# Attention with values split into halves: the low halves from a TensorE product and a ScalarE copy instead of a VectorE subtraction

## Chip, cores and metric

One core of one Trainium2 chip. The metric is the device time of one execution in microseconds (us), the median of several runs. The engines of the core are named as the profile does: PE (TensorE), DVE (VectorE), ACT (ScalarE), POOL (GpSimd), SP (SyncE).

## What is computed

The reference runs four blocks on x of shape (4, 2048, 256); the second and fourth are the same feed-forward block, the third is the attention that the change is in:

```python
x = x + attn_a(layernorm(x))          # row 1 of each sequence, one 256x256 product, broadcast
x = x + ffn(layernorm(x))             # sigmoid(xr Wr) * (relu(xk Wk)^2 Wv), x mixed with the row before
x = x + attn_b(layernorm(x))          # below
x = x + ffn(layernorm(x))
# attn_b: 16 heads of 64, windows of 128 rows
q, k, v = rope(proj(Wq, bq)), rope(proj(Wk, bk)), proj(Wv, bv)
kcat, vcat = (window before, own window)
scores = q kcat^T / 8, masked to kj >= qi and kj <= qi + 128
ctx = softmax(scores) vcat
out = merged(ctx) Wo^T + bo
```

Products of float32 values are made from float16 halves: a value is split into a high half (rounded to float16) and a low half (what is left, again float16), and three products (high-high, high-low, low-high) are summed in PSUM. The values v are such a case. The high half is `v_h`, the low half `v_l = v - v_h`.

## The kernel before

The kernel has three stages on one core: a feed-forward stage (which also prepares the attention's weights), the attention, and a second feed-forward stage. Everything is ordered by hand: every engine has a function `at_step(t)` that lists its pieces in the order in which it issues them, and semaphores alone tie the engines together. Each engine runs its list strictly in order, so a wait holds up all that stands behind it.

The attention has 64 steps t. A step is one group of 4 heads (g = t % 4) for one big block S = t // 4 of 4 x 128 rows; 16 big blocks make 4 sequences of 4. For a step and each block b of its four, the pieces are:

- queries and keys: `project` on PE (L1580) into one of the two banks `pr_ps[:, half]`; then the rotary products by `key_product`, `query_product` (DVE L1341, L1351 and POOL), the copies `key_copy`, `query_copy` (ACT L1504, L1514), and the sums on POOL (L1171, L1181).
- values: `values` on PE (L1597) into the same two banks, `v_high_of` on ACT (L1475) writes the high half, `v_low_of` on DVE (L1330) the low half. Both read the bank.
- scores on PE (L1685), `tops` on DVE (L1256, masks the scores and takes the maximum of a row), `exponentials` on ACT (L1457), `p_high_of` on ACT (L1466) and `p_low_of` on DVE (L1268) for the halves of the probabilities, a DMA transpose (`turn_p`, L1061), `values_product` on PE (L1638 to L1640), `context` on DVE (L1277, L1283).
- context: `context_high` on ACT (L1495), its low half on POOL (L1202), a DMA transpose (L1069), `output` on PE (L1654, L1657), `residual` on DVE (L1320).
- every fourth step: row statistics on DVE (`moments`, in steps with g = 1 and g = 3), and with g = 3 `normalize` and `x_high_of` on ACT (L1522, L1533) and `x_low_of` on DVE (L1312) for the block after next.

In step t the engines work on the scores of step t, on values and queries of step t + 1, and on keys of step t + 2. The two banks `pr_ps[:, 0]` and `pr_ps[:, 1]` are shared: queries, then values, then keys go through both. `keys_of(t + 2, half)` may overwrite a bank only when the low half of the values has been read from it:

```python
def keys_of(t, half):
    ...
    pe.wait_ge(xt_in[r], xt_ready(t // NG))
    need(v_low[half], t)
    project(r, KC + t % NG * 2 * P, half, k_done[half])
```

The order of PE in `at_step(t)` around it is: values of t + 1, `values_product(t - 1, 3)`, `output(t - 5)`, `values_product(t, 0)`, `keys_of(t + 2, 1)`, `scores(t + 1, 0)`, `keys_of(t + 2, 0)`, `values_product(t, 1)`. DVE's is: `tops(t, 3)`, `context(t - 1, 3)`, `v_low_of(t + 1, 1)`, `residual(t - 5)`, `v_low_of(t + 1, 0)`, `context(t, 0)`, two key products of t + 2 (they wait for `keys_of(t + 2, 1)`), `p_low_of(t, 2)`, `p_low_of(t, 3)`. ACT's is: `exponentials(t, 3)`, with g = 3 `normalize` and `x_high_of`, `p_high_of(t, 3)`, `context_high(t - 1)`, `key_copy(t + 2)`.

Of the kernel before, what the change touches and what calls it, by code (L numbers as in the profile page):

```python
# [57 lines left out]
def identity(nc, pool, tile, made, n=1):  # L58
# [21 lines left out]
             "kt": F + 57376, "prob": F + 69664, "v_h": F + 77856, "v_l": F + 84096, "halves": F + 90240,  # L80
             "pt": F + 106624, "c_halves": F + 114816, "tables": D, "masks": D + 8192, "rows": D + 10240,
             "bias_parts": D + 10496, "out_bias": D + 11008}
# [784 lines left out]
def attention_stage(nc, stack, x_in, x_out, place, banks, pre, past, bv, bo, cos, sin):  # L867
# [34 lines left out]
    out_bias = sb("out_bias", [P, C])  # L902
    masks = sb("masks", [P, 2 * P])
    rows = sb("rows", [P, P], BF16)
    bias_parts = sb("bias_parts", [P, C], BF16)
# [61 lines left out]
    k_carried = sem("k_carried")  # L967
    v_high = [sem("v_first_high"), sem("v_second_high")]
    v_low = [sem("v_first_low"), sem("v_second_low")]
    s_done = sem("s_done")  # L970
# [13 lines left out]

    MASKS_MADE, MADE = 5, 6
    OUT_BIAS_MADE = 11
# [155 lines left out]
    def gpsimd(pool):  # L1142
# [62 lines left out]
        def opening():  # L1205
# [8 lines left out]
            for half, rule in enumerate((beyond, until)):  # L1214
                part = masks[:, half * P:(half + 1) * P]
                nc.gpsimd.affine_select(out=part, in_=part, **rule).then_inc(made, 1)

        def first_std():
# [25 lines left out]
    def vector(dve):  # L1244
# [77 lines left out]

        def v_low_of(t, half):

            if step(t):
                dve.wait_ge(v_high[half], t + 1)
                if t < 2:
                    dve.wait_ge(past.act_made, 2 * past.CHUNKS)
                at = pair_of(t, half)
                nc.vector.tensor_tensor(v_l[:, at, :, :],  # L1330
                                        pr_ps[:, half, :].rearrange("p (b h d) -> p b h d", b=2, d=HD),
                                        v_h[:, at, :, 0:HD], ALU.subtract).then_inc(v_low[half], 1)

        def key_product(t, n):
# [58 lines left out]
        def at_step(t):  # L1393
# [15 lines left out]
            context(t - 1, 3)  # L1409
            v_low_of(t + 1, 1)  # L1410
            if g == 3 and S > -2:
                shift_of(S + 2)
            residual(t - 5)
            v_low_of(t + 1, 0)
            context(t, 0)
# [31 lines left out]
    def scalar(act):  # L1447
# [21 lines left out]
        def v_high_of(t, half):  # L1469

            if step(t):
                act.wait_ge(v_done[half], t + 1)
                need(pv_done, 4 * t - 4)
                at = pair_of(t, half)
                nc.scalar.activation(v_h[:, at, :, 0:HD],  # L1475
                                     pr_ps[:, half, :].rearrange("p (b h d) -> p b h d", b=2, d=HD),
                                     ACT.Copy).then_inc(v_high[half], 1)

        def carry_keys(t):
# [59 lines left out]
        def at_step(t):  # L1539
# [14 lines left out]
            if g == 3 and S > -2:  # L1554
                x_high_of(S + 2)
            p_high_of(t, 3)
            context_high(t - 1)
            key_copy(t + 2)
# [3 lines left out]
    def tensor(pe):  # L1562
# [22 lines left out]
        def values(t, half):  # L1585

            if step(t):
# [6 lines left out]
                for blk in range(2):  # L1594
                    for n, (xp, wp) in enumerate(TERMS):
                        for k in range(CK):
                            last = nc.tensor.matmul(  # L1597
                                pr_ps[:, half, blk * 2 * P:(blk + 1) * 2 * P], xt[:, r, xp, 2 * half + blk, k, :],
                                w[wp][:, k, VC + g * 2 * P:VC + (g + 1) * 2 * P],
                                start=n == 0 and k == 0, stop=n == 2 and k == CK - 1)  # L1600
                last.then_inc(v_done[half], 1)

        def keys_of(t, half):
# [87 lines left out]
        def at_step(t):  # L1691
# [6 lines left out]
            values_product(t - 1, 3)  # L1698
            output(t - 5)
            values_product(t, 0)  # L1700
            keys_of(t + 2, 1)
# [207 lines left out]
```

## Time and profile before

| | |
|---|---|
| median of 3 runs | 1657.75 us (1651.25 to 1658.65) |
| profiled execution | 1650.62 us |
| its span | 1648.8 us |
| its mean granted clock of PE | 0.981 |
| PE, PE's weight loads | 1487.5 us (90%), 1125.5 us (68%) |
| DVE | 1458.6 us (88%) |
| ACT | 1262.6 us (77%) |
| POOL | 967.5 us (59%) |

The span is what the profiler saw between first and last instruction; the profiled execution's own time is 1.8 us longer. Busy times are shares of the whole span, in which the attention takes about the stretch from 210 to 1450 us. A group of instructions carries a count, its busy time, the mean of one, and the idle time of its engine just before it with what ended it. In an order of time a row with x4 is four instructions run together. The durations of two instructions in a row can overlap a little, so a distance between starts is often the better measure.

### The profile page before, as it was taken

The numbers are of one execution on the slowest core, as the hardware profiler recorded it, in microseconds if no ns is written. First come the engines' busy times: TensorE is split into PE (matmuls) and PEld (weight loads), VectorE is DVE, ScalarE is ACT, GpSimd is POOL, SyncE is SP. The second block draws the span as 40 slices with busy tenths as digits, with TensorE's granted clock in tenths as the row PEclk, the third lists the DMA queues.
The fourth block names the chain that finished last, engine by engine and source line by source line (L and its number), as shares of the span: only waits on it lengthen the run. The fifth ranks groups of instructions, "written<-read, shape, count | busy, mean of one in ns | idle before, by whom it ended". The sixth has DMA issues, their size and how long they took to land. (4 is left out here: it accounts for less than half of the span.)

```text
span 1648.8 us, 46118 instructions
## 1 busy us (share of the span) xinstructions
PE 1487.5 (90%) x16674; PEld 1125.5 (68%) x16674; DVE 1458.6 (88%) x4009; ACT 1262.6 (77%) x2266; POOL 967.5 (59%) x786
## 2 busy tenths in 40 slices
PE   5999978899989999999989999999998999869998
PEld 4888745566666676666667666666666666658887
DVE  5999588899989999999999999999999989957885
ACT  5999567777767787877777877778787767749996
POOL 4665357565656666656666665666676656513443
PEclk7999999999999999999999999999999999979999
DMA  5233247899899989899999989899999798971331
GB/s 208 91 121 106 77 91 129 163 152 180 147 175 157 179 164 179 163 169 171 166 180 156 183 155 181 151 181 164 179 159 176 155 154 153 171 169 61 111 112 73
DMA packets 721528, 247.86 MB, mean 150 GB/s; under 512 B 687380, under 2 KB 706072, under 8 KB 721304
## 3 DMA queue, kind: packets, MB, share of 16 engines
q1 hardware_dynamic: 720600, 244.53, 76.4%
q8 instruction: 135, 2.21, 0.5%
q14 instruction: 89, 0.73, 0.1%
q10 hardware_dynamic: 704, 0.40, 0.1%
HBM read 47.73 MB, written 25.17 MB: 44 GB/s over the span
## 5 line engine op out<-in xcount | busy, mean ns | idle before, releaser
L1457 ACT ACTIVATE at_prob<-at_prob,at_top 128x256 f32<-128x256 f32 (+1 forms) x1024 | 429.0, 490 | 104.4 <-DVE at_top L1256 101.1
L1256 DVE CUSTOM_DVE_ANT_0 at_prob<-banks,at_masks,pre_s_scale 128x256 f32<-128x256 f32 (+1 forms) x1024 | 420.3, 470 | 16.2 <-PE banks L1685 1.9
L1268 DVE TENSOR_TENSOR at_halves<-at_prob,at_halves 128x1024 f16<-128x1024 f32 (+1 forms) x256 | 306.2, 1212 | 0.7 <-ACT at_halves L1466 0.7
L1580 PE MATMUL banks<-at_xt,pre_w_h 128*128 128x512 f16 x1024 | 297.9, 383 | 4.8 <-DVE at_v_l L1330 4.2
L1685 PE MATMUL banks<-at_kt,at_qt 32*128 32x256 f32 (+1 forms) x4096 | 253.8, 384 | 52.1 <-DVE at_top L1256 21.1
L1202 POOL TENSOR_TENSOR at_c_halves<-at_ctx,at_c_halves 128x1024 f16<-128x1024 f32 x64 | 136.6, 2135 | 267.0 <-DVE at_halves L1268 261.4
L1685 PEld LDWEIGHTS banks<-at_kt,at_qt 32*128 32x128 f32 x4096 | 202.5, 187 | 112.8 <-issue 110.5
L1466 ACT ACTIVATE at_halves<-at_prob 128x1024 f16<-128x1024 f32 (+1 forms) x256 | 263.6, 1030 | 7.7
L1638 PE MATMUL banks<-at_v_h,at_pt 128*128 128x65 f16 x1984 | 208.0, 195 | 49.8 <-DMA at_pt<-at_halves 32.8
L1638 PEld LDWEIGHTS banks<-at_v_h,at_pt 128*128 128x128 f16 x1984 | 181.1, 97 | 104.1 <-issue 49.3
L1171 POOL TENSOR_TENSOR at_kt<-at_k_by 128x512 f32<-128x512 f32 x128 | 163.0, 1274 | 94.4 <-DVE at_halves L1268 94.3
L1161 POOL TENSOR_TENSOR at_q_by<-at_q_first,at_tables 128x512 f32<-128x512 f32 x128 | 163.1, 1275 | 81.0 <-DVE at_halves L1268 81.0
L1639 PE MATMUL banks<-at_v_l,at_pt 128*128 128x64 f16 x1984 | 207.6, 193 | 0.0
L1640 PE MATMUL banks<-at_v_h,at_pt 128*128 128x65 f16 x1984 | 207.4, 194 | 0.0
L1639 PEld LDWEIGHTS banks<-at_v_l,at_pt 128*128 128x128 f16 x1984 | 182.1, 99 | 6.8
L1504 ACT ACTIVATE at_k_first<-banks,pre_bias 128x512 f32<-128x512 f32 x64 | 44.0, 687 | 186.2 <-PE banks L1580 186.2
L1640 PEld LDWEIGHTS banks<-at_v_h,at_pt 128*128 128x128 f16 x1984 | 182.5, 98 | 0.0
L325 POOL TENSOR_TENSOR f_x<-f_x,f_gated 128x512 f32<-128x512 f32 x64 | 83.1, 1308 | 156.1 <-DVE f_gated L430 156.1
L1151 POOL TENSOR_TENSOR at_k_by<-at_k_first,at_tables 128x512 f32<-128x512 f32 x128 | 160.5, 1276 | 13.8 <-ACT at_k_first L1504 13.8
L1597 PE MATMUL banks<-pre_w_h,at_xt 128*128 128x256 f16 x1024 | 164.1, 273 | 0.8 <-ACT at_q_first L1514 0.8
L1181 POOL TENSOR_TENSOR at_qt<-at_q_by 128x512 f32<-128x512 f32 x128 | 160.2, 1273 | 0.0
L1580 PEld LDWEIGHTS banks<-at_xt,pre_w_h 128*128 128x128 f16 x1024 | 87.1, 98 | 104.7 <-issue 28.8
(124 smaller groups left out, 3221.0 us busy)
## 6 DMA issues: line engine op xcount, KB each, us to landing
f_x<-in_x SPq DMA_DIRECT2D x16, 512.0 KB, 4.0
x_after_ffn<-f_x SPq DMA_DIRECT2D x16, 512.0 KB, 2.6
at_x_ln<-x_after_ffn SPq DMA_DIRECT2D x16, 512.0 KB, 4.7
at_x_res<-x_after_ffn SPq DMA_DIRECT2D x64, 128.0 KB, 2.9
x_after_attention<-at_x_res SPq DMA_DIRECT2D x64, 128.0 KB, 2.7
f_x<-x_after_attention SPq DMA_DIRECT2D x16, 512.0 KB, 4.3
out_x<-f_x SPq DMA_DIRECT2D x16, 512.0 KB, 3.0
at_tables<-in_cos SPq DMA_DIRECT2D x16, 256.0 KB, 3.7
```

The costliest lines, as they stand in the source:

```text
L1161: nc.gpsimd.tensor_tensor(q_by[:, n, :], q_first[:, :], tables[:, r, n // 3, :], ALU.mult).then_inc(q_made[n], 1)
L1171: nc.gpsimd.tensor_tensor(kt[:, half, own(t, 0):own(t, 0) + SB, :].rearrange("p s t -> p (s t)"), k_by[:, 2 * half, :], k_by[:, 2 * half + ...
L1256: last = nc.vector.tensor_tensor_reduce(out=prob[:, n % 2, h, low:2 * P], in0=s_ps[:, h, n % 2 * 2 * P + low:(n % 2 + 1) * 2 * P], in1=mas ...
L1268: nc.vector.tensor_tensor(parts[:, 1, :, :], prob[:, n % 2, :, keys_from(t, b):2 * P], parts[:, 0, :, :], ALU.subtract).then_inc(p_low, 1)
L1457: last = nc.scalar.activation(at, at, ACT.Exp, bias=top[:, n % 2, h:h + 1], scale=-1.0)
L1466: nc.scalar.activation(halves_of(n, alone(t, b))[:, 0, :, :], prob[:, n % 2, :, keys_from(t, b):2 * P], ACT.Copy).then_inc(p_high, 1)
L1580: last = nc.tensor.matmul(pr_ps[:, half, :].rearrange("p (b t) -> p b t", b=SB), w[wp][:, k, at:at + P], xt[:, r, xp, :, k, :], start=n == ...
L1597: last = nc.tensor.matmul(pr_ps[:, half, blk * 2 * P:(blk + 1) * 2 * P], xt[:, r, xp, 2 * half + blk, k, :], w[wp][:, k, VC + g * 2 * P:VC ...
L1638: nc.tensor.matmul(out, ph, v_h[:, at, h, :], start=s == 0, stop=False)
L1639: nc.tensor.matmul(out[:, 0:HD], ph, v_l[:, at, h, :], start=False, stop=False)
L1640: last = nc.tensor.matmul(out, pl, v_h[:, at, h, :], start=False, stop=s == len(slots) - 1)
L1685: last = nc.tensor.matmul(s_ps[:, h, d * 2 * P + keys_from(t, b):(d + 1) * 2 * P] .rearrange("p (s t) -> p s t", t=P), qt[rows_of, par, ha ...
```

## The change

The low half is made by PE in the bank itself: after the values' sum has been copied out as `v_h`, a product of minus the identity (`neg_eye`, float16, made once on POOL) with `v_h` is added to the same sum, so that the bank holds v - v_h. ACT then copies the bank to `v_l`. The subtraction on DVE is gone. `values` no longer closes its sum, and starts it only once for the bank.

```diff
+    neg_eye = sb("neg_eye", [P, P], F16)
...
+    v_rest = [sem("v_first_rest"), sem("v_second_rest")]
...
-    MASKS_MADE, MADE = 5, 6
+    MASKS_MADE, EYE_MADE, MADE = 5, 7, 8
...
+            nc.gpsimd.memset(neg_eye[:, :], 0.0).then_inc(made, 1)
+            pool.wait_ge(made, EYE_MADE - 1)
+            nc.gpsimd.affine_select(out=neg_eye[:, :], in_=neg_eye[:, :], compare_op=ALU.not_equal, fill=-1.0, base=0,
+                                    pattern=[[-1, P]], channel_multiplier=1).then_inc(made, 1)
...
-        def v_low_of(t, half):
-
-            if step(t):
-                dve.wait_ge(v_high[half], t + 1)
...
-                nc.vector.tensor_tensor(v_l[:, at, :, :],
-                                        pr_ps[:, half, :].rearrange("p (b h d) -> p b h d", b=2, d=HD),
-                                        v_h[:, at, :, 0:HD], ALU.subtract).then_inc(v_low[half], 1)
...
             context(t - 1, 3)
-            v_low_of(t + 1, 1)
             if g == 3 and S > -2:
                 shift_of(S + 2)
             residual(t - 5)
-            v_low_of(t + 1, 0)
             context(t, 0)
...
+        def v_low_of(t, half):
+
+            if step(t):
+                act.wait_ge(v_rest[half], t + 1)
...
+                nc.scalar.activation(v_l[:, pair_of(t, half), :, :],
+                                     pr_ps[:, half, :].rearrange("p (b h d) -> p b h d", b=2, d=HD),
+                                     ACT.Copy).then_inc(v_low[half], 1)
...
             p_high_of(t, 3)
+            v_low_of(t + 1, 1)
+            v_low_of(t + 1, 0)
             context_high(t - 1)
             key_copy(t + 2)
...
-                                start=n == 0 and k == 0, stop=n == 2 and k == CK - 1)
+                                start=blk == 0 and n == 0 and k == 0, stop=False, skip_group_check=True)
...
+        def values_rest(t, half):
+
+            if step(t):
+                pe.wait_ge(v_high[half], t + 1)
...
+                for blk in range(2):
+                    last = nc.tensor.matmul(
+                        pr_ps[:, half, blk * 2 * P:(blk + 1) * 2 * P].rearrange("p (h d) -> p h d", d=HD),
+                        neg_eye[:, :], v_h[:, valued(t, 2 * half + blk), :, 0:HD], start=False, stop=blk == 1,
+                        skip_group_check=True)
+                last.then_inc(v_rest[half], 1)
...
             output(t - 5)
+            values_rest(t + 1, 1)
+            values_rest(t + 1, 0)
             values_product(t, 0)
             keys_of(t + 2, 1)
```

How the order of the instructions moves, with the semaphores that each waits for. ACT in a step with g = 3, before (L1457 exponentials, L1522 and L1533 x, L1466 high half of block 3, L1495 context, L1504 keys):

```order
L1457 ACTIVATE at_prob<-at_prob,at_top 128x256 [waits at_top_made]
L1457 ACTIVATE at_prob<-at_prob,at_top 128x256 x3
L1522 ACTIVATE at_x_ln<-at_x_ln,at_shift,at_rstd 128x256 [waits at_shift_made]
L1522 ACTIVATE at_x_ln<-at_x_ln,at_shift,at_rstd 128x256 x3
L1533 ACTIVATE at_x_halves<-at_x_ln 128x1024 [waits at_xt_in0,at_xn_made]
L1466 ACTIVATE at_halves<-at_prob 128x1024 [waits at_pt_in1,at_p_made]
L1495 ACTIVATE at_c_halves<-at_ctx 128x1024 [waits at_ct_in,at_ctx_made]
L1504 ACTIVATE at_k_first<-banks,pre_bias 128x512 [waits at_k_product3,at_k_product0,at_k_first_done]
```

And the same place of the change, whose lines have other numbers (the low halves are L1478):

```order
L1450 ACTIVATE at_prob<-at_prob,at_top 128x256 [waits at_top_made]
L1450 ACTIVATE at_prob<-at_prob,at_top 128x256 x3
L1525 ACTIVATE at_x_ln<-at_x_ln,at_shift,at_rstd 128x256 [waits at_shift_made]
L1525 ACTIVATE at_x_ln<-at_x_ln,at_shift,at_rstd 128x256 x3
L1536 ACTIVATE at_x_halves<-at_x_ln 128x1024 [waits at_xt_in0,at_xn_made]
L1459 ACTIVATE at_halves<-at_prob 128x1024 [waits at_pt_in1,at_p_made]
L1478 ACTIVATE at_v_l<-banks 128x2x256 [waits at_v_second_rest]
L1478 ACTIVATE at_v_l<-banks 128x512 [waits at_v_first_rest]
L1498 ACTIVATE at_c_halves<-at_ctx 128x1024 [waits at_ct_in,at_ctx_made]
L1507 ACTIVATE at_k_first<-banks,pre_bias 128x512 [waits at_k_product3,at_k_product0,at_k_first_done]
```

The two copies stand behind the high half of block 3, and in such a step behind the normalizing too; nothing else moved. PE from the output to the keys' first projection, before; the rest of the context's products is left out:

```order
L1657 MATMUL banks<-pre_wo_h,pre_raw 128x256 x8
L1638 MATMUL banks<-at_v_h,at_pt 128x65 [waits at_v_second_low,at_ctx_made,at_v_first_low,at_pt_in0]
L1639 MATMUL banks<-at_v_l,at_pt 128x64
L1640 MATMUL banks<-at_v_h,at_pt 128x65
...
L1580 MATMUL banks<-at_xt,pre_w_h 128x512 [waits at_v_second_low,at_xt_in1]
```

The same place of the change (L1675 is the output, L1656 to L1658 are the context's products):

```order
L1675 MATMUL banks<-pre_wo_h,pre_raw 128x256 x8
L1675 MATMUL banks<-pre_wo_l,pre_raw 128x256 x8
L1675 MATMUL banks<-pre_wo_h,pre_raw 128x256 x8
L1615 MATMUL banks<-at_v_h,at_neg_eye 128x256 [waits at_v_second_high]
L1615 MATMUL banks<-at_v_h,at_neg_eye 128x256
L1615 MATMUL banks<-at_v_h,at_neg_eye 128x256 [waits at_v_first_high]
L1615 MATMUL banks<-at_v_h,at_neg_eye 128x256
L1656 MATMUL banks<-at_v_h,at_pt 128x65 [waits at_v_second_low,at_ctx_made,at_v_first_low,at_pt_in0]
L1657 MATMUL banks<-at_v_l,at_pt 128x64
L1658 MATMUL banks<-at_v_h,at_pt 128x65
...
L1585 MATMUL banks<-at_xt,pre_w_h 128x512 [waits at_v_second_low,at_xt_in1]
```

Four products are put in ahead of the context's products; the keys' projection waits for the same semaphore as before, which ACT now raises. On DVE the key products follow the context of block 0 as before, without the two subtractions:

```order
L1289 TENSOR_TENSOR at_ctx<-banks,at_inv 128x256 [waits at_ct_low,at_inv_made]
L1326 SCALAR_TENSOR_TENSOR at_x_res<-banks,pre_o_down,at_x_res 128x256 [waits at_res_in0,at_o_done]
L1283 RECIPROCAL at_inv<-banks 128x4 [waits at_pv_done]
L1289 TENSOR_TENSOR at_ctx<-banks,at_inv 128x256 [waits at_ct_low,at_inv_made]
L1336 SCALAR_TENSOR_TENSOR at_k_by<-banks,pre_bias,at_tables 128x512 [waits at_k_first_roped,at_k_second_done,at_tab_in0]
L1336 SCALAR_TENSOR_TENSOR at_k_by<-banks,pre_bias,at_tables 128x512 [waits at_k_second_roped,at_k_second_done,at_tab_in0]
L1274 TENSOR_TENSOR at_halves<-at_prob,at_halves 128x1024 [waits at_p_high] x2
```

The key products (L1336) still wait for the keys' projection into the second bank, and the last two low halves of the probabilities (L1274) stand behind them.

## Rows read from the trace of the kernel before

**Rows 1.** The page, first part: busy time, share and instructions of each engine.
```profile
PE 1487.5 (90%) x16674; PEld 1125.5 (68%) x16674; DVE 1458.6 (88%) x4009; ACT 1262.6 (77%) x2266; POOL 967.5 (59%) x786
```

**Rows 2.** Busy time by stretch (start:end, length, each engine, PEclk, DMA share, GB/s).
```profile
700.00:900.00 200.00, 183.77 (x2382) 132.26 (x2384) 188.06 (x558) 150.06 (x275) 127.33 (x98) 1.00 0.95 167
```

**Rows 3.** Waits of PE and DVE, 220 to 1430 us: us in total, times, longest.
```profile
PE banks L1638 <- DMA at_pt<-at_halves: 29.7, 29, 3.4
PE banks L1580 <- DVE at_v_l L1330: 2.7, 1, 2.7
...
DVE at_k_by L1341 <- PE banks L1580: 21.6, 46, 2.0
```

**Rows 4.** The two tiles of the halves: min/median/max ns, first and last start.
```profile
L1330 DVE TENSOR_TENSOR at_v_l<-banks,at_v_h x128: 672/679/692, 210.1 to 1431.0; 128x512 f16<-128x512 f32 x128
...
L1475 ACT ACTIVATE at_v_h<-banks x128: 580/590/599, 209.5 to 1429.1; 128x512 f16<-128x512 f32 x128
```

**Rows 5.** Order of time on DVE around 738 us (start, length, line).
```profile
737.51 0.68 DVE L1330 TENSOR_TENSOR at_v_l<-banks,at_v_h 128x512 f16<-128x512 f32 x1
...
738.50 0.68 DVE L1330 TENSOR_TENSOR at_v_l<-banks,at_v_h 128x512 f16<-128x512 f32 x1
...
740.01 1.41 DVE L1341 SCALAR_TENSOR_TENSOR at_k_by<-banks,pre_bias,at_tables 128x512 f32<-128x512 f32 x2 [0.28 <-PE banks L1580]
```

**Rows 6.** Order of time on ACT, the same step.
```profile
737.07 1.71 ACT L1457 ACTIVATE at_prob<-at_prob,at_top 128x256 f32<-128x256 f32 x4
738.81 1.06 ACT L1466 ACTIVATE at_halves<-at_prob 128x1024 f16<-128x1024 f32 x1
739.77 1.04 ACT L1495 ACTIVATE at_c_halves<-at_ctx 128x1024 f16<-128x1024 f32 x1
```

**Rows 7.** Order of time on PE, the same step: output, then the keys.
```profile
735.77 1.04 PE L1657 MATMUL banks<-pre_wo_l,pre_raw 128*128 128x256 f16 x8
736.64 1.04 PE L1657 MATMUL banks<-pre_wo_h,pre_raw 128*128 128x256 f16 x8
...
738.45 0.60 PE L1580 MATMUL banks<-at_xt,pre_w_h 128*128 128x512 f16 x2
```

**Rows 8.** DVE: key products of single steps, and statistics of two rows.
```profile
680.86 1.41 DVE L1341 SCALAR_TENSOR_TENSOR at_k_by<-banks,pre_bias,at_tables 128x512 f32<-128x512 f32 x2
...
700.40 1.41 DVE L1341 SCALAR_TENSOR_TENSOR at_k_by<-banks,pre_bias,at_tables 128x512 f32<-128x512 f32 x2 [0.29 <-PE banks L1580]
...
711.19 0.75 DVE L1292 BATCH_NORM_STATS2 at_stats<-at_x_ln 128x6 f32<-128x256 f32 x2
...
711.97 0.25 DVE L1297 BATCH_NORM_AGGREGATE at_mv<-at_stats 128x2 f32<-128x6 f32 x2
...
721.61 1.41 DVE L1341 SCALAR_TENSOR_TENSOR at_k_by<-banks,pre_bias,at_tables 128x512 f32<-128x512 f32 x2 [0.44 <-PE banks L1580]
...
759.11 1.41 DVE L1341 SCALAR_TENSOR_TENSOR at_k_by<-banks,pre_bias,at_tables 128x512 f32<-128x512 f32 x2
...
875.40 1.41 DVE L1341 SCALAR_TENSOR_TENSOR at_k_by<-banks,pre_bias,at_tables 128x512 f32<-128x512 f32 x2
```

**Rows 9.** ACT: the last high half of single steps.
```profile
699.20 1.06 ACT L1466 ACTIVATE at_halves<-at_prob 128x1024 f16<-128x1024 f32 x1
...
719.23 1.06 ACT L1466 ACTIVATE at_halves<-at_prob 128x1024 f16<-128x1024 f32 x1
...
760.84 1.04 ACT L1466 ACTIVATE at_halves<-at_prob 128x1024 f16<-128x1024 f32 x1
...
891.60 1.06 ACT L1466 ACTIVATE at_halves<-at_prob 128x1024 f16<-128x1024 f32 x1
```

**Rows 10.** The line of the key products, 210 to 1440 us.
```profile
L1341 DVE SCALAR_TENSOR_TENSOR at_k_by<-banks,pre_bias,at_tables x126: 735/743/753, 213.0 to 1414.8; 128x512 f32<-128x512 f32 x126
```

**Rows 11.** Busy time by stretch, where the clock falls.
```profile
1328.00:1332.00 4.00, 1.82 (x33) 1.36 (x30) 3.79 (x15) 3.85 (x9) 2.84 (x3) 1.00 1.40 203
1332.00:1336.00 4.00, 3.10 (x15) 2.25 (x16) 0.98 (x2) 3.57 (x6) 3.01 (x3) 0.58 0.92 215
```

More of the change, by code:

```diff
@@ L80 @@
              "kt": F + 57376, "prob": F + 69664, "v_h": F + 77856, "v_l": F + 84096, "halves": F + 90240,
-             "pt": F + 106624, "c_halves": F + 114816, "tables": D, "masks": D + 8192, "rows": D + 10240,
+             "pt": F + 106624, "c_halves": F + 114816, "tables": D, "masks": D + 8192, "neg_eye": D + 9216, "rows": D + 10240,
              "bias_parts": D + 10496, "out_bias": D + 11008}
@@ L1321, in residual @@
                                                x_res[:, i % RB, :], ALU.mult, ALU.add).then_inc(x_made, 1)
-        def v_low_of(t, half):
-            if step(t):
-                dve.wait_ge(v_high[half], t + 1)
-                if t < 2:
-                    dve.wait_ge(past.act_made, 2 * past.CHUNKS)
-                at = pair_of(t, half)
-                nc.vector.tensor_tensor(v_l[:, at, :, :],
-                                        pr_ps[:, half, :].rearrange("p (b h d) -> p b h d", b=2, d=HD),
-                                        v_h[:, at, :, 0:HD], ALU.subtract).then_inc(v_low[half], 1)
         def key_product(t, n):
@@ L1477, in v_high_of @@
                                      ACT.Copy).then_inc(v_high[half], 1)
+        def v_low_of(t, half):
+            if step(t):
+                act.wait_ge(v_rest[half], t + 1)
+                if t < 2:
+                    act.wait_ge(past.act_made, 2 * past.CHUNKS)
+                nc.scalar.activation(v_l[:, pair_of(t, half), :, :],
+                                     pr_ps[:, half, :].rearrange("p (b h d) -> p b h d", b=2, d=HD),
+                                     ACT.Copy).then_inc(v_low[half], 1)
         def carry_keys(t):
@@ L1599, in values @@
                                 w[wp][:, k, VC + g * 2 * P:VC + (g + 1) * 2 * P],
-                                start=n == 0 and k == 0, stop=n == 2 and k == CK - 1)
+                                start=blk == 0 and n == 0 and k == 0, stop=False, skip_group_check=True)
                 last.then_inc(v_done[half], 1)
+        def values_rest(t, half):
+            if step(t):
+                pe.wait_ge(v_high[half], t + 1)
+                if t == 0:
+                    pe.wait_ge(made, EYE_MADE)
+                for blk in range(2):
[4 more added lines that the diff above has]
+                last.then_inc(v_rest[half], 1)
         def keys_of(t, half):
```

## Prediction

> **What bounds the kernel now.** I read the page's busy times first, then a stretch of the attention, then the waits, and last the order of time inside single steps. On the page TensorE (PE) and VectorE (DVE) are close, 90% and 88% of the span; ScalarE (ACT) has 77% [rows 1]. Inside the attention, of 200 us PE works 184, DVE 188, ACT 150 [rows 2]: VectorE is the fullest, PE next. PE's waits end mostly on DMA transposes of the probabilities (29.7 us), and only once, for 2.7 us, on the low halves of the values; DVE's longest wait, 21.6 us, is for the keys' projection [rows 3]. Two engines are nearly full, so the question is which ring of waits closes first when work leaves one of them.
>
> The ring to look at runs through the accumulation banks: the keys of the step after next are projected into the bank that the values have just left. In the quiet step around 738 us DVE writes the second half's low part at 737.51 and the first half's at 738.50, and its key product starts at 740.01 [rows 5]. PE starts the last products of the output at 736.64 and the keys' first projection at 738.45 [rows 7]. ACT is then still at the exponentials of the last block (from 737.07) and at its high half (from 738.81); only at 739.77 does it take the next thing [rows 6]. The low half that the projection needs was ready at 737.51 + 0.68 = 738.19, before PE asked for it.
>
> **The change, part by part.** *VectorE loses* two subtractions a step in 64 steps: 0.679 us each by their median [rows 4], about 0.6 from start to next start. That is 1.2 us a step, 77 us if VectorE alone set the pace. *TensorE gains* four products of 128x256 a step. Eight such take 736.64 - 735.77 = 0.87 us, 0.109 each [rows 7]: 0.44 us a step, 28 us in all, placed behind the output. *ScalarE gains* two copies of the shape of the high halves, 0.590 us each [rows 4], about 1.1 us a step, 70 in all; it idles 50 us in 200, about ten steps [rows 2]. By busy time alone that is a fair trade. The minus identity is made once on GpSimd in the first stage, where GpSimd is not full (59% of the span) [rows 1]; I take 0, and at worst it is two small operations of 1 us each, if a stage should wait for them.
>
> *What moves is the moment at which the bank is free.* The copies stand on ACT behind the high half of block 3. So the keys' first projection now waits for this chain: VectorE's last maxima, four exponentials, in every fourth step four normalizing operations and the high half of x as well, the high half of block 3, the copy. Behind the projection on PE stand the scores of the next step. Behind the key product on VectorE stand both last low halves of the probabilities and all maxima of the next step, and the last of these starts the exponentials again. It is a closed ring of engines that work in order, and its length is a floor for the step.
>
> *Length of one round*, from key product to key product. From there to the start of the last high half I take what the trace has, since nothing that is removed lies in it: 738.81 - 721.61 = 17.20 us in a quiet step [rows 6, 8]. Then the tail: high half to ACT's next start, 739.77 - 738.81 = 0.96 [rows 6]; the copy, 0.59 [rows 4]; the hand-over to PE, 0.10 (an estimate, the one thing not in a row); projection to key product, 740.01 - 738.45 = 1.56 [rows 5, 7]. Tail 3.21, round **20.41 us**, where before it took 740.01 - 721.61 = 18.40 [rows 5, 8]. The other steps of a group of four have, up to the high half: 699.20 - 680.86 = 18.34 (with x's low half, 1.14 more than 17.20), 719.23 - 700.40 = 18.83 (with statistics of two rows, 0.95 from 711.19 to their end; the rest is a wait), and 760.84 - 740.01 = 20.83 (statistics, normalizing and x's high half, 3.63 more) [rows 8, 9]. A group is 17.20 + 18.34 + 18.83 + 20.83 + 4 x 3.21 = 88.0 us, or 87.4 without that wait, against 759.11 - 680.86 = 78.25 before: **9.1 to 9.8 us more per four steps**.
>
> *Over the attention.* Key products run from 213.0 to the last pair, 0.7 us before 1414.8 [rows 10]: 62 rounds, 1201.1 us. After: 62 x 20.41 = 1265.4; 14 groups with the extras, each 1.14 + 0.95 + 3.63 = 5.72, make 80.1; the 16 steps that open a sequence are shorter by 17.20 - (891.60 - 875.40) = 1.0 each [rows 8, 9]. Sum 1265.4 + 80.1 - 16 = 1329.5, so **+128.4 us**. PE's four new products are not in it: PE comes to the bank some 2 us before ACT frees it, and they hide there; if that cover went, they would cost their 28 us. Nor are the DMAs in it: SyncE and GpSimd keep their order, every transpose keeps its distance to the key product and has a later reader.
>
> *Added terms.* The first copy, behind normalizing too: 3 us, as in any long step less what starts late anyway. Rounds with the statistics of two rows, where PE already came late and now has 0.44 us more: 14 x 0.3, 4 us. TensorE's clock: PE's wait will be some 5 us in the 14 long steps. Where PE was busy 1.82 us of 4, the granted clock of the next 4 us was 0.58, so at 1.2 GHz most of it, a loss of (1 - 0.58) x 4 = 1.7 us [rows 11]. A projection at 1.2 GHz takes 1.3 us longer and lies in the ring. The bounds are 0 and twice that loss, 3.4 us a long step, 48 in all; I take less than one such loss, since part of it falls into the wait itself: 14 x 1.1 = 15 us. The Trainium skill, "TensorE: Matmul & The Clock Gate", section "Why this matters for your kernels", asks for no long idle gap between bursts of matmuls, since the clock then falls back. By it this term is there in every long step; by the stretch of rows 2 (clock 1.00 with PE idle 16 of 200 us) it would be nearly 0.
>
> Sum: 128 + 3 + 4 + 15 = 150 on the profiled execution's 1650.6 us, 1801. That execution is 7 us under the median of the runs, 1657.75, whose spread is 7.4; I add half of that: **1804 us**, 8.8% slower.
>
> **Rivals.**
> *A, the old waits stay on top.* Each round keeps the waits it has and adds its own shift: 739.77 + 0.59 + 0.10 + 1.56 - 740.01 = 2.01 in a quiet step, 760.84 + 3.21 - 759.11 = 4.94 in a long one. 48 x 2.01 + 14 x 4.94 = 166; with start, clock and products 188, and the 3 us towards the median: 1842. For it: the DMA share is 0.95 [rows 2]. Against: those waits hang on work behind the key product, and every round now gives that work 2 us more room.
> *B, the clock stays low* for much of a round after each long wait. PE works 184 of 200 us [rows 2], about 18 a step; 8 us of that at half speed add 8, of which VectorE's own work covers perhaps half: 14 x 4 = 56 in place of 15, 1845. Against: one low stretch was enough to recover [rows 11].
> *C, faster.* The ring is not what decides, because ACT gets to its last high half earlier than I hold. Then VectorE gives 77 us, and PE, idle for 8% of 1201 us, 96, can follow for 96 - 28 = 68: 1590 at best counted from the median, at half of it 1624. It decides once the ring is more than 2.0 us shorter than mine. Against: ACT's last exponentials start at 737.07 [rows 6], 0.44 before VectorE's subtraction at 737.51 [rows 5], which stands only two small operations behind the last maxima; there is nothing ahead of them to save. The Trainium skill, "Perfetto Trace Analysis", section "Identifying the Most-Contended Engine", says to work first on the engine with the highest occupancy; here that is VectorE, so by the page this relief should pay.
> *D, no change:* the ring is not closed in the program, for instance if the copy of the second half stood ahead of the high half. The order on ACT shows it behind. 1650 to 1662.
>
> **How the numbers follow.** Forecast 0.76, A 0.13, B 0.05, C 0.03, D 0.03. About 0.5%, 8 us, is what a measurement of this kernel can tell from no change. The range: its floor is 1650.6 + 128 less 8 for rounds that come out a little shorter, 1771; its top takes in the clock's upper end, 1804 + 33 = 1837, and A's 1842: 1771 to 1842. Slower by over 0.5% 0.94, within 0.5% 0.03, faster 0.03.
>
> **What would show it.** PE idle ahead of the keys' first projection, ended by ACT's copy, about 2 us in quiet steps and 5 in long ones; VectorE idle ahead of the key product by as much and by the 1.2 us it was relieved of, ended by PE; key products 20.4 us apart in quiet steps; waits on transposes mostly gone; stretches of the attention with a granted clock under 1. If key products stay 18 us apart, the ring does not decide and the prediction is wrong in kind; if PE's wait is there and the time grows by less than 100 us, the tail or the count of rounds is wrong.

## The result, and the profile after

The changed kernel takes 1826.36 us (median of 4 runs, 1822.41 to 1827.26); the kernel before 1656.97 us beside it. The ratio is 1.102, with a 95% interval of 1.099 to 1.106: 169 us more. The profiled execution took 1827.03 us, its span is 1825.2 us, so 176.4 us more span than before.

Busy times on the page of the changed kernel, to be read against [rows 1], and one stretch of the attention against [rows 2]:

```profile
PE 1561.8 (86%) x16930; PEld 1169.2 (64%) x16930; DVE 1398.0 (77%) x3881; ACT 1324.6 (73%) x2394; POOL 968.5 (53%) x788
```

```profile
700.00:900.00 200.00, 171.34 (x2127) 122.11 (x2125) 156.25 (x462) 142.41 (x260) 110.17 (x85) 0.96 0.85 149
```

VectorE is lighter by 61 us and from the fullest engine of the attention has become one that idles 44 us in 200. PE is busy 74 us longer, far more than four products a step (28 us): part of its work ran at the low clock, for the granted clock of this stretch is 0.96 and was 1.00. No engine is full now. The waits of PE and of DVE from 220 to 1610 us (against [rows 3]) show where the engines stood instead (us in total, times, longest):

```profile
PE banks L1585 <- ACT at_v_l L1478: 124.3, 55, 5.1
PE banks L1703 <- DVE at_top L1262: 36.1, 55, 5.8
PE banks L1672 <- DMA pre_raw<-at_c_halves: 18.5, 14, 3.1
PE banks L1656 <- DMA at_pt<-at_halves: 16.6, 20, 2.0
...
DVE at_k_by L1336 <- PE banks L1585: 199.8, 62, 7.0
```

PE waits 124 us for ScalarE's copy ahead of the keys' projection (L1585), where it waited once for 2.7 us before; VectorE waits 200 us for that projection ahead of its key product, where it waited 21.6. The key products, the same view as [rows 8], show the rounds:

```profile
710.25 1.41 DVE L1336 SCALAR_TENSOR_TENSOR at_k_by<-banks,pre_bias,at_tables 128x512 f32<-128x512 f32 x2 [1.38 <-PE banks L1585]
...
730.69 1.41 DVE L1336 SCALAR_TENSOR_TENSOR at_k_by<-banks,pre_bias,at_tables 128x512 f32<-128x512 f32 x2 [2.52 <-PE banks L1585]
...
756.00 1.41 DVE L1336 SCALAR_TENSOR_TENSOR at_k_by<-banks,pre_bias,at_tables 128x512 f32<-128x512 f32 x2 [6.90 <-PE banks L1585]
...
777.57 1.41 DVE L1336 SCALAR_TENSOR_TENSOR at_k_by<-banks,pre_bias,at_tables 128x512 f32<-128x512 f32 x2 [1.65 <-PE banks L1585]
```

The quiet round is 730.69 - 710.25 = 20.44 us. The long one, with ScalarE's normalizing in it, is 25.31, and the one behind it, with x's low half on VectorE, 21.57. In the quiet one the tail reads off ACT and PE, against [rows 6, 7]:

```profile
727.46 1.06 ACT L1459 ACTIVATE at_halves<-at_prob 128x1024 f16<-128x1024 f32 x1
728.42 1.07 ACT L1478 ACTIVATE at_v_l<-banks 128x512 f16<-128x512 f32 x2
```

```profile
729.14 0.59 PE L1585 MATMUL banks<-at_xt,pre_w_h 128*128 128x512 f16 x2 [1.65 <-ACT at_v_l L1478]
```

From the high half at 727.46 to the key product at 730.69 it is 3.23 us, in the order of the sum: 0.96 to the copy, 0.72 for the copy with the hand-over, 1.55 for the projection. In the long step the same place of PE looks so:

```profile
746.61 0.61 PE L1615 MATMUL banks<-at_v_h,at_neg_eye 128*128 128x256 f16 x4
753.18 1.01 PE L1585 MATMUL banks<-at_xt,pre_w_h 128*128 128x512 f16 x2 [4.79 <-ACT at_v_l L1478]
...
755.83 3.00 PE L1703 MATMUL banks<-at_kt,at_qt 32*128 32x256 f32 x32
```

The four products with minus the identity take 0.61 us run together and are done 6 us before they are needed. PE then idles 4.79 us, and the projection that ends the wait runs at the low level: two products take 1.01 us, not 0.59, and to the key product it is 2.82 us, not 1.55. The stretch that it stands in has a granted clock of 0.50, 1.2 GHz, behind one in which PE was busy 0.40 us of 4:

```profile
748.00:752.00 4.00, 0.40 (x14) 0.27 (x10) 1.06 (x4) 3.97 (x8) 2.58 (x3) 0.88 0.10 22
752.00:756.00 4.00, 2.81 (x10) 0.90 (x11) 0.01 (x1) 2.47 (x4) 0.00 (x0) 0.50 0.00 0
```

Over the attention, the line of the key products (against [rows 10]):

```profile
L1336 DVE SCALAR_TENSOR_TENSOR at_k_by<-banks,pre_bias,at_tables x126: 740/746/753, 218.5 to 1591.7; 128x512 f32<-128x512 f32 x126
```

62 rounds take 1591.0 - 218.5 = 1372.5 us, 171.4 more than before; the first begins 5.5 us later. Within 0.5 us that is the whole 176.4.

### The profile page after: what moved, and what is told of

It is laid out like the page before. It is cut to its first block and busy times, and to the rows that moved or that the text cites. A ratio compares the mean times of both kernels' runs of the same rounds, so it can differ in the third digit from the quotient of the medians.

```text
span 1825.2 us, 46635 instructions
## 1 busy us (share of the span) xinstructions
PE 1561.8 (86%) x16930; PEld 1169.2 (64%) x16930; DVE 1398.0 (77%) x3881; ACT 1324.6 (73%) x2394; POOL 968.5 (53%) x788
## 5 line engine op out<-in xcount | busy, mean ns | idle before, releaser
L1585 PE MATMUL banks<-at_xt,pre_w_h 128*128 128x512 f16 x1024 | 312.1, 399 | 130.0 <-ACT at_v_l L1478 129.6
L1274 DVE TENSOR_TENSOR at_halves<-at_prob,at_halves 128x1024 f16<-128x1024 f32 (+1 forms) x256 | 305.9, 1211 | 0.7 <-ACT at_halves L1459 0.7
L1703 PE MATMUL banks<-at_kt,at_qt 32*128 32x256 f32 (+1 forms) x4096 | 270.8, 404 | 40.6 <-DVE at_top L1262 38.8
L1703 PEld LDWEIGHTS banks<-at_kt,at_qt 32*128 32x128 f32 x4096 | 211.8, 201 | 112.8 <-issue 104.9
L1336 DVE SCALAR_TENSOR_TENSOR at_k_by<-banks,pre_bias,at_tables 128x512 f32<-128x512 f32 x128 | 90.2, 746 | 209.5 <-PE banks L1585 209.5
L1585 PEld LDWEIGHTS banks<-at_xt,pre_w_h 128*128 128x128 f16 x1024 | 88.7, 100 | 240.2 <-issue 167.8
L1656 PE MATMUL banks<-at_v_h,at_pt 128*128 128x65 f16 x1984 | 208.6, 195 | 26.9 <-DMA at_pt<-at_halves 19.1
L1656 PEld LDWEIGHTS banks<-at_v_h,at_pt 128*128 128x128 f16 x1984 | 181.8, 98 | 75.2 <-issue 37.5
L1658 PE MATMUL banks<-at_v_h,at_pt 128*128 128x65 f16 x1984 | 208.0, 194 | 0.0
L1658 PEld LDWEIGHTS banks<-at_v_h,at_pt 128*128 128x128 f16 x1984 | 182.9, 98 | 0.0
```

Source lines behind the costliest of these rows:

```text
L1274: nc.vector.tensor_tensor(parts[:, 1, :, :], prob[:, n % 2, :, keys_from(t, b):2 * P], parts[:, 0, :, :], ALU.subtract).then_inc(p_low, 1)
L1585: last = nc.tensor.matmul(pr_ps[:, half, :].rearrange("p (b t) -> p b t", b=SB), w[wp][:, k, at:at + P], xt[:, r, xp, :, k, :], start=n == ...
L1656: nc.tensor.matmul(out, ph, v_h[:, at, h, :], start=s == 0, stop=False)
L1658: last = nc.tensor.matmul(out, pl, v_h[:, at, h, :], start=False, stop=s == len(slots) - 1)
L1703: last = nc.tensor.matmul(s_ps[:, h, d * 2 * P + keys_from(t, b):(d + 1) * 2 * P] .rearrange("p (s t) -> p s t", t=P), qt[rows_of, par, ha ...
```

## The experiments

Theory: the *ring* (exponentials, high half, copy on ScalarE, keys' projection, key product, maxima) sets the time by its length, and it is closed by the place of the second bank's copy. Rivals: the *added work* on TensorE and ScalarE, or *copies and products in these banks* as such, cost the 169 us. A second question is why lightening VectorE gave nothing. All ratios are to the kernel before.

### The same work, the copies further ahead on ScalarE

```diff
             exponentials(t, 3)
+            v_low_of(t + 1, 1)
+            v_low_of(t + 1, 0)
             if g == 3 and S > -2:
                 normalize(S + 2)
...
             p_high_of(t, 3)
-            v_low_of(t + 1, 1)
-            v_low_of(t + 1, 0)
```

> The change, with ScalarE's two copies moved: they stand right behind the exponentials of block 3 and ahead of normalizing and of the high half of block 3; the work is the same on every engine. Ring theory: the quiet round loses the high half's 0.96 us (20.44 to about 19.45), the long one 3.9 us and its slow projection too; 62 rounds give about 1229 us in place of 1372, so about 1695 us. If the cost is the added work (70 us on ScalarE, 28 us on TensorE) or a slower use of the banks, the time stays at about 1826 us.

1705.61 us, ratio 1.029 (1.027 to 1.031). Moving two calls gives back 121 of the 169 us with every instruction kept. The added work is not what costs. A long round, from key product to key product, is now 20.03 us in place of 25.31:

```profile
680.79 1.41 DVE L1336 SCALAR_TENSOR_TENSOR at_k_by<-banks,pre_bias,at_tables 128x512 f32<-128x512 f32 x2 [1.43 <-PE banks L1585]
700.82 1.41 DVE L1336 SCALAR_TENSOR_TENSOR at_k_by<-banks,pre_bias,at_tables 128x512 f32<-128x512 f32 x2 [1.63 <-PE banks L1585]
```

The quiet round before it (661.44 to 680.79) is 19.35 us, a little shorter than the 19.45 expected. What is left of the cost, 48 us, goes with a ring that is still 0.95 us longer than the 18.40 of before.

### No products

```diff
-            values_rest(t + 1, 1)
-            values_rest(t + 1, 0)
...
-                act.wait_ge(v_rest[half], t + 1)
+                act.wait_ge(v_high[half], t + 1)
```

In this kernel `values` starts and closes its sum itself again.

> The change without TensorE's products with minus the identity; ScalarE's copies wait for the high halves and so copy v itself (the low half is not what it should be). Ring theory: the products are hidden in TensorE's wait, so 1810 to 1826 us, the difference being the few places where a copy waited for them (11 us). TensorE-work theory: at least 28 us less, below 1798 us.

1830.63 us, ratio 1.104 (1.101 to 1.107), the same as the change within the noise, and 4 us above the range that I had named. 256 products less give nothing: they lay in PE's wait. No gain shows either from the few waits of the copies for them.

### Only one of the two halves

In both hybrids one bank's low half is the subtraction on VectorE at its old place and the other's is product and copy. `v_low_by_subtraction` is the old subtraction, and `values` closes the sum of the bank that it reads. Second bank subtracted (the lines are of VectorE, ScalarE and TensorE, in this order):

```diff
             context(t - 1, 3)
+            v_low_by_subtraction(t + 1, 1)
...
-            v_low_of(t + 1, 1)
...
-            values_rest(t + 1, 1)
```

> Hybrid: the second bank's low half, for which the first projection of the keys waits, is VectorE's subtraction again at its old place; only the first bank's goes by product and copy at the place of the change. Ring theory: the first projection is as early as before, the second has 3 us of room behind the scores, VectorE is 0.6 us a step lighter: 1635 to 1660 us. If the cost is in any copy on ScalarE or any product on TensorE, half of the 169 us stays: about 1740 us.

First bank subtracted (the same edit with 0, behind `residual`):

> The other hybrid: the first bank's low half is subtracted by VectorE again, the second bank's goes by product and copy. Ring theory: the ring runs through the second bank alone, so it stays at 1815 to 1830 us. If each half carries its share, about 1740 us.

Second bank subtracted: 1670.76 us, ratio 1.008 (1.006 to 1.009). First bank subtracted: 1830.82 us, 1.104 (1.102 to 1.107). One of two like copies carries all of it: the one in the bank into which the keys are projected first. But the good hybrid is 13 us slower than before, outside of what I expected, though VectorE is 0.6 us a step lighter. That opened the second question.

### The long steps alone

```diff
+            p_high_of(t, 3)
+            v_low_of(t + 1, 1)
+            v_low_of(t + 1, 0)
             if g == 3 and S > -2:
                 normalize(S + 2)
             if g == 3 and S > -2:
                 x_high_of(S + 2)
-            p_high_of(t, 3)
-            v_low_of(t + 1, 1)
-            v_low_of(t + 1, 0)
```

> The change with ScalarE's normalizing and the high half of x moved behind the two copies; in quiet steps nothing differs. Ring theory: a long round loses 2.7 us of normalizing and high half and the 1.25 us of the slow projection, 25.3 to 21.4, in 14 rounds: 55 us less, about 1770 us, and quiet rounds stay at 20.44. If the long rounds are slow for another reason, less than 20 us is gained.

1763.57 us, ratio 1.064 (1.062 to 1.067): 63 us less than the change. Its key products, first a quiet round and then a long one:

```profile
766.78 1.41 DVE L1336 SCALAR_TENSOR_TENSOR at_k_by<-banks,pre_bias,at_tables 128x512 f32<-128x512 f32 x2 [1.06 <-PE banks L1585]
787.23 1.41 DVE L1336 SCALAR_TENSOR_TENSOR at_k_by<-banks,pre_bias,at_tables 128x512 f32<-128x512 f32 x2 [2.51 <-PE banks L1585]
809.20 1.41 DVE L1336 SCALAR_TENSOR_TENSOR at_k_by<-banks,pre_bias,at_tables 128x512 f32<-128x512 f32 x2 [3.57 <-PE banks L1585]
```

The quiet round is 20.45 us, as before the edit; the long one is 21.97 in place of 25.31. Over the trace the 14 long rounds are 2.9 to 4.2 us shorter than in the change, 50 us together. I had expected 3.9 of each, with a projection at the full clock in all of them. In 6 of the 14 it was so, and three of these rounds took 21.13 us; in the other 8, the one shown among them, the projection still ran at the low level at least in part. The ring's length follows what is put on it.

### Filling TensorE's wait

```diff
-                for h in range(GROUP):
+                long = b == 0 and t % NG == 3 and t // NG + 2 < NS
+                for h in [h for _ in range(6 if long else 1) for h in range(GROUP)]:
```

> The change, with the products of probabilities and values of block 0 made six times over in the 14 long steps, each time from the start, so the result is the same: 5 x 24 products, about 3.7 us of TensorE's wait of 5 us ahead of the keys' projection are filled. Clock theory: the granted clock stays at 1.00 in those steps, the projection takes 1.56 and not 2.81 us to the key product, 14 x 1.25 = 17 us less, about 1808 us. If the long steps are slow for another reason, about 1826 us or more.

1814.46 us, ratio 1.094 (1.092 to 1.096): 12 us less, where 17 were expected, by 1440 products more. That is 10 x 120 and 4 x 60, since four of the 14 steps open a sequence and have half the keys in block 0. In one long step with 120 more:

```profile
725.77 1.41 DVE L1336 SCALAR_TENSOR_TENSOR at_k_by<-banks,pre_bias,at_tables 128x512 f32<-128x512 f32 x2 [2.52 <-PE banks L1585]
749.81 1.41 DVE L1336 SCALAR_TENSOR_TENSOR at_k_by<-banks,pre_bias,at_tables 128x512 f32<-128x512 f32 x2 [2.05 <-PE banks L1585]
```

```profile
744.00:748.00 4.00, 3.08 (x103) 2.96 (x99) 0.61 (x2) 3.97 (x7) 1.68 (x2) 1.00 0.14 32
748.00:752.00 4.00, 3.74 (x40) 2.27 (x41) 2.19 (x3) 1.54 (x3) 0.00 (x0) 1.00 0.00 0
```

The clock stays at 1.00, and the long round is 24.04 us, the one worked out before without a clock term (20.83 + 3.21). In the trace the projection runs at the full level in 11 of the 14 long steps. In three, all of them with 60 products more, PE still idles 3.3 us and the projection is at the low level as in the change; the later two of these rounds (from 635.87 and from 987.39 us) take 24.31 us, where the same two took 24.29 and 24.30 in the change. 11 x 1.25 is 14 us, near the 12 measured. The clock's price of 1.25 us a long round is shown.

### Why a lighter VectorE gains nothing

First the kernel before with the subtraction simply left out. The low halves are not made; in their place TensorE multiplies by the high halves once more, and it waits for those:

```diff
-            v_low_of(t + 1, 1)
...
-            v_low_of(t + 1, 0)
...
-                need(v_low[half], t)
+                need(v_high[half], t)
...
-                        nc.tensor.matmul(out[:, 0:HD], ph, v_l[:, at, h, :], start=False, stop=False)
+                        nc.tensor.matmul(out[:, 0:HD], ph, v_h[:, at, h, 0:HD], start=False, stop=False)
```

> The kernel before without the subtraction and without its place in the order: the low halves of the values are not made, TensorE takes the high halves in their place and waits for those. Second-ring theory (TensorE from the scores of the second pair of blocks to the keys' projection, then VectorE from the key product to the maxima of block 1, which frees the scores' banks; the subtraction is not on it, VectorE waits there anyway): 1640 to 1658 us. If VectorE alone set the pace, its 77 us go: 1580 to 1600 us.

1661.75 us, ratio 1.002 (1.000 to 1.003), 4 us above the range that I had named: no gain for 77 us of VectorE's work. The rows of a quiet round in it, VectorE's key products and its context of block 3:

```profile
720.74 1.41 DVE L1341 SCALAR_TENSOR_TENSOR at_k_by<-banks,pre_bias,at_tables 128x512 f32<-128x512 f32 x2 [0.71 <-PE banks L1578]
...
736.32 0.42 DVE L1283 TENSOR_TENSOR at_ctx<-banks,at_inv 128x256 f32<-128x256 f32 x1
...
739.16 1.41 DVE L1341 SCALAR_TENSOR_TENSOR at_k_by<-banks,pre_bias,at_tables 128x512 f32<-128x512 f32 x2 [0.71 <-PE banks L1578]
```

PE's scores of the second pair of blocks, the end of its output, and its first product for the context of block 0:

```profile
727.81 2.01 PE L1685 MATMUL banks<-at_kt,at_qt 32*128 32x256 f32 x32 [0.50 <-DVE at_top L1256]
...
735.79 1.04 PE L1657 MATMUL banks<-pre_wo_h,pre_raw 128*128 128x256 f16 x8
736.89 0.19 PE L1638 MATMUL banks<-at_v_h,at_pt 128*128 128x65 f16 x1
```

The round is 18.42 us; it was 18.40 with the subtraction. VectorE waits 0.71 us for the keys' projection, PE 0.50 us for the maxima that free the scores' bank. That is the second ring that I had in mind: VectorE from the key product over two low halves to the maxima of block 1 (720.74 to 727.81, 7.07 us), then PE over scores, values, output and context to the keys' projection and the key product (727.81 to 739.16, 11.35 us).

These 11.35 us hold one more wait. The output's last products begin at 735.79 and take 0.87 us, to 736.66, but the products for the context of block 0 begin only at 736.89. VectorE's context of block 3 ends at 736.74, and PE goes on 0.15 us behind it. The kernel before has the same place, with the same 0.15 us (737.16 + 0.42 = 737.58, then 737.74), while its output, begun at 736.64 [rows 7], was done at 737.51:

```profile
737.16 0.42 DVE L1283 TENSOR_TENSOR at_ctx<-banks,at_inv 128x256 f32<-128x256 f32 x1
```

```profile
737.74 0.19 PE L1638 MATMUL banks<-at_v_h,at_pt 128*128 128x65 f16 x1
```

So what closes a quiet round is a cycle close beside it: VectorE's own list from the key product to the context of block 3, 16.0 us in which the trace shows no wait for another engine, the hand-over, 0.15, and PE's products of block 0 with the keys' projection up to the key product, 2.27 (736.89 to 739.16). My second ring is 0.2 us shorter. On both, the subtractions do not lie: they stand on VectorE behind the context of block 3, where VectorE waits for PE anyway.

If so, work added on PE ahead of that place costs what goes beyond 0.2 us, though PE idles 8%. Four more products in the output, each written over by the next:

```diff
-                nc.tensor.matmul(o_ps[:, 0:C], rows[:, :], bias_parts[:, :], start=True, stop=False)
+                for n in range(5):
+                    nc.tensor.matmul(o_ps[:, 0:C], rows[:, :], bias_parts[:, :], start=True, stop=n < 4)
```

> The kernel before with four more products of 128x256 in each step's output on TensorE, each overwriting the other, at 0.109 us each, with no new wait. Second-ring theory: they lie on the ring, 64 x 0.44 = 28 us less what the few waits of TensorE there take up: 1675 to 1685 us. If VectorE alone set the pace they hide in TensorE's 8% of idle time: 1655 to 1660 us.

1672.27 us, ratio 1.009 (1.006 to 1.011): 12 us, less than half of the 28 expected and far more than nothing. Most quiet rounds take 18.64 us (from 805.89 to 824.52, for one, 18.63), 0.24 more than before: of the four products' 0.44 us the first 0.2 fall into PE's wait. The long rounds stay at 19.1; there PE waited 0.9 us for VectorE's context of block 3, and the products are covered. So my second ring is there, but one through more of VectorE's own work lies 0.2 us above it and takes part of the load.

The change's products with the copies on VectorE, where `v_low_copied` is a plain copy from the bank behind `v_rest`:

```diff
             residual(t - 5)
+            v_low_copied(t + 1, 1)
+            v_low_copied(t + 1, 0)
             context(t, 0)
```

> The change, with the two copies on VectorE behind the residual instead of on ScalarE: TensorE's products stay. Second-ring theory: the four products are on the ring with 0.44 us, and the residual and a copy stand between the output and the projection with some 0.5 us: 1680 to 1720 us. Theory that the products themselves cost the 169 us: about 1826 us.

1699.39 us, ratio 1.024 (1.022 to 1.027), as expected. The bank is free later than with the subtraction, which needed neither output nor residual ahead of it, and still 127 us of the change's cost are gone.

The good hybrid with its products moved out of the second ring:

```diff
-            values_rest(t + 1, 0)
             values_product(t, 0)
             keys_of(t + 2, 1)
+            values_rest(t + 1, 0)
             scores(t + 1, 0)
```

> The hybrid with the second bank's subtraction, but TensorE's two products for the first bank stand behind the first projection of the keys, outside the second ring. Second-ring theory: quiet rounds back to the 18.2 us of before, 1650 to 1663 us, where the other hybrid has 1671. If the 13 us came from ScalarE's copy, it stays at 1671 us.

1662.81 us, ratio 1.004 (1.002 to 1.006), where the hybrid had 1.008 (1.006 to 1.009): 8 us less in the medians, with intervals that just touch. A quiet round:

```profile
724.11 1.41 DVE L1347 SCALAR_TENSOR_TENSOR at_k_by<-banks,pre_bias,at_tables 128x512 f32<-128x512 f32 x2 [0.71 <-PE banks L1596]
...
742.51 1.41 DVE L1347 SCALAR_TENSOR_TENSOR at_k_by<-banks,pre_bias,at_tables 128x512 f32<-128x512 f32 x2 [0.71 <-PE banks L1596]
```

It takes 18.40 us, and the hybrid's quiet round took 18.42 (728.09 to 746.51): two products, 0.22 us, had fitted into PE's wait of 0.2. The quiet rounds never grew by the two products, and the 8 us are no sign of the ring. Of the hybrid's 62 rounds, 16 us longer in the trace than before, 10 lie in the rounds with the statistics of two rows, where PE waits on transposes and which the traces of all these kernels show between 20 and 26 us. Why they are longer there stays open.

### Shortening the second ring

On TensorE and VectorE of the kernel before:

```diff
-            values_product(t, 0)
             keys_of(t + 2, 1)
+            values_product(t, 0)
             scores(t + 1, 0)
...
+            v_low_of(t + 1, 1)
             context(t - 1, 3)
-            v_low_of(t + 1, 1)
...
-            context(t, 0)
             key_product(t + 2, 1)
             key_product(t + 2, 2)
+            context(t, 0)
```

> The kernel before with the keys' first projection ahead of the context's products of block 0 on TensorE, and on VectorE the second bank's subtraction ahead of the context of block 3 and both key products ahead of the context of block 0. Second-ring theory: the ring loses 0.73 us on TensorE and gains 0.54 on VectorE, a quiet round is 18.0 to 18.2 us, 1640 to 1660 us. If VectorE's own work sets the pace, no change: 1655 to 1662 us.

> The same order, with the first bank's low half by product (behind the first projection) and copy, so that VectorE is 0.6 us a step lighter. Second-ring theory: as the one with that order alone, 1640 to 1660 us, within 5 us of it. If VectorE's own work is next in line once the ring is shorter, it is 10 us or more below that one.

The new order alone: 1640.73 us, ratio 0.990 (0.988 to 0.993), 1% faster than the kernel before and the fastest of all. With the first bank's low half by product and copy on top: 1648.78 us, 0.994 (0.992 to 0.997). Both beat both kernels. The second is 8 us above the first and not within 5 as expected; the idea of the change has nothing to give here. A quiet round of the new order, and PE's projection in it:

```profile
633.24 1.41 DVE L1341 SCALAR_TENSOR_TENSOR at_k_by<-banks,pre_bias,at_tables 128x512 f32<-128x512 f32 x2 [0.27 <-issue]
...
649.15 0.68 DVE L1330 TENSOR_TENSOR at_v_l<-banks,at_v_h 128x512 f16<-128x512 f32 x1
...
651.53 1.41 DVE L1341 SCALAR_TENSOR_TENSOR at_k_by<-banks,pre_bias,at_tables 128x512 f32<-128x512 f32 x2 [0.16 <-issue]
```

```profile
649.98 0.59 PE L1580 MATMUL banks<-at_xt,pre_w_h 128*128 128x512 f16 x2
```

It is 18.29 us. The cycle through VectorE's own list now ends with the second bank's subtraction (649.83), and the projection follows 0.15 us behind. Against before it has lost PE's products of block 0, 0.72 us, and VectorE's part, which now holds the subtraction, and block 0's context in place of block 3's, is 0.61 longer: 18.40 - 0.72 + 0.61 = 18.29. The quiet round of the hybrid in this order is 18.30 (719.92 to 738.22), the same, since the subtraction that it saves is the first bank's, which stands behind that place. These rounds explain only a part of the gain: in the traces the 62 rounds are 5 us shorter than before (1196.0 against 1201.1), in the medians the kernel is 16 us faster. The rest is not explained; the products, too, shift against their transposes in this order, and I did not part the two.

## Why the prediction was right, and where its sizes were off

The prediction was 1804 us, range 1771 to 1842; 1826 came. The mechanism is the one forecast, and single rounds hold to a few hundredths. The forecast had 150 us on the profiled execution, which took 176 more: of the 26 missing some 14 are the start, 8 the rounds with statistics, 2 the clock of the long steps and 2 a miscount: the first two rounds also hold x's low half and statistics, which the 14 groups left out. The 3 us added towards the median did not come (1827.0 in the profiled execution, 1826.4 in the median), and by this luck the forecast misses by 22 and not by 26.

- *The tail, 3.21 us.* Measured 3.23. The hand-over, estimated at 0.10, was 0.13 (0.72 less 0.59). The quiet round came out at 20.44 for 20.41.
- *The long round.* 25.31 us measured; 24.04 forecast plus 1.25 for the clock, and the filled kernel shows 24.04.
- *62 rounds.* 1372.5 us against a floor of 1329.5. The 43 us above it are: 13 long rounds with the slow projection, 17; 14 rounds with two rows' statistics, in which PE came late, 12 above the 21.36 forecast for them (one, from 866 to 890 us, took 24.01); the first five rounds, 12, and the 2 of the miscount.
- *TensorE's clock, 15 us.* The size was right for the long steps. The rule of the Trainium skill ("TensorE: Matmul & The Clock Gate", section "Why this matters for your kernels"), which asks for no long idle gap, agrees with the trace in every long step: PE idle 4.8 to 5.1 us, then 0.50. The other reading, that nothing would come of it, failed. Not forecast was that the projection also ran at the low level in the first five rounds, behind waits of 1.9 to 4.9 us: about 6 of their 12 us.
- *Rounds with the statistics of two rows, 4 us.* Almost 12 us came on top of that in 14 rounds. The statistics cost less than held (21.10 less 20.44, 0.66 for 0.95), and five of the rounds lost 1.6 to 4.2 us. There PE waits for the transposed context (18.5 us in 14 waits for `pre_raw`, 15.8 in 14 before) and for the probabilities (16.6 us, 29.7 before), and I had let the 2 us of new room cover that; together these waits went from 45.5 to 35.1 us and were not mostly gone. Rival A, which keeps all of them, gives these rounds 23.1 us on average (21.1 before and its 2.0), the forecast 21.1; they took 22.0. Both are off by about 1. In the total A, at 1842, was 16 us too high and the forecast 22 too low, so the number alone would not decide for the forecast.
- *The start, 3 us, is the term most off*: 5.5 us for the first copy with its slow projection, and the 12 in the first five rounds, where the granted clock was 0.59 (212 to 220 us) and 0.57 (228 to 236 us).
- *Four new products hide in PE's wait.* Right: leaving them out gave nothing. The price named for a lost cover, 28 us, was not met in the nearest case measured: in the kernel before, four more products a step cost 12 us.
- *VectorE's 77 us.* Rival C took 34 to 68 us for the relief if the new ring were not there. Measured, it is zero. What I had missed is where the subtractions stand in the round of the kernel before: in the 2.4 us in which VectorE waits for PE. The Trainium skill ("Perfetto Trace Analysis", section "Identifying the Most-Contended Engine") would have us work on the fullest engine first. Here the fullest, at 188 of 200 us, holds 16.0 of the cycle's 18.4 us, and yet it could lose two operations a step without a measurable effect: occupancy named the engine, and not which of its work counts.

## What to carry to other kernels

When the engines work in order and are tied by semaphores, follow a cycle from one instruction to the same instruction of the next step, across engines, and add it up from starts in the trace: its length is a floor, and work off the cycle was worth nothing here, though its engine was the fullest. Look for waits inside the parts before you call a cycle the bound: two cycles here lay 0.2 us apart. An instruction that frees a shared PSUM bank belongs at the earliest place of its engine's list; before moving such a step to an idler engine, look at what stands ahead of it there. And of two equal pieces of work only the one on the cycle counted here, so a change can often be kept for the one and undone for the other.

## What I had not expected of the hardware

At first sight the products do not all slow down alike at the low clock. The projection went from 1.55 to 2.82 us up to the key product, nearly its double, but the 32 products of the scores behind it, with 32 rows each in float32, took 3.00 us, where the same group takes 2.01 at the full clock (the row at 727.81 above), half as much again. The granted clock explains it: it was 0.50 up to 757.5 us, 0.60 in the next half microsecond and 1.00 from 758.0 on. So some 2.1 of the 3.00 us were at half speed, worth 1.05, and 0.9 at full speed, together 1.95, close to the 2.01. The level can change in the middle of a group, so a group's factor is read only beside the clock in a finer stretch.

The clock was also low behind short waits at the start of the attention: the projection at 332.45 us took 1.01 us for two products behind a wait of 1.87 us, while behind 1.65 us in the later quiet rounds it took 0.59.
